# The second layer's routed experts inside the mixed stage, with stores that add their rows in memory

## The reference, cut to what matters

```python
x = x + _L0_attn_ref(xn, ...) + _L0_ffn_ref(xn, ...)
xn = _layernorm(x, axis=-1)
x = x + _L1_attn_ref(xn, ...) + _L1_ffn_ref(xn, ...)

# _L1_ffn_ref
gates = softmax(logits)                      # 8 experts
idx = argmax(gates)
locations = cumsum(mask1, axis=0) - mask1    # place of the token in its expert
mask1 = mask1 * (locations < capacity)       # capacity = 8192 / 8 = 1024
h = gelu(einsum('ecm,emi->eci', dispatched, inter_w) + inter_b)
expert_out = einsum('eci,eim->ecm', h, output_w) + output_b
moe_out = einsum('sec,ecm->sm', combine, expert_out)
out = res_mlp_out * coef[:, :1] + moe_out * coef[:, 1:] + residual
```

## Time and profile before

| | us |
|---|---|
| median of 3 runs | 1391.96 |
| lowest and highest | 1389.64, 1392.7 |
| the profiled execution | 1388.63 |
| its span in the trace | 1386.8 |

### The profile page before, as it was taken

The page is one execution under the profiler, slowest core; times in us unless marked ns, Lnnn a source line. Parts: engine busy times, 40 slices in busy tenths (PEclk is TensorE's granted clock), DMA queues, the critical chain, the costliest instruction groups (busy, mean ns, idle before and its releaser), DMA issues. The chain is left out here.

```text
span 1386.8 us, 28532 instructions
## 1 busy us (share of the span) xinstructions
PE 1158.3 (84%) x9562; PEld 856.0 (62%) x9562; DVE 1009.0 (73%) x3197; ACT 684.5 (49%) x1151; POOL 552.4 (40%) x524
## 2 busy tenths in 40 slices
PE   0771599999999997999999988999599899679980
PEld 0550255555555544899999885777366667579970
DVE  7905899999999994667666654888654688657753
ACT  1751277777777775444444334555332455334430
POOL 2300133333333331555555451333368477235550
PEclk9885699999999998999999998999799999889995
DMA  9252400000000001222222212224166000312218
GB/s 316 118 193 58 170 25 23 25 25 23 25 26 25 23 25 31 66 69 69 71 69 70 64 58 79 62 62 137 51 218 201 17 30 28 137 54 69 67 57 242
DMA packets 97340, 110.26 MB, mean 80 GB/s; under 512 B 13340, under 2 KB 84700, under 8 KB 96988
## 3 DMA queue, kind: packets, MB, share of 16 engines
q1 hardware_dynamic: 75264, 77.23, 17.7%
q0 software_dynamic: 12800, 26.63, 5.7%
q10 hardware_dynamic: 9180, 5.14, 1.2%
HBM read 59.71 MB, written 49.25 MB: 79 GB/s over the span
## 5 line engine op out<-in xcount | busy, mean ns | idle before, releaser
L1029 POOL DMA_INDIRECT slots<-rowbuf,slots x192 | 193.7, 1009 | 354.9 <-ACT probs L841 335.4
L1139 POOL DMA_INDIRECT y<-slot_y,where x208 | 217.8, 1047 | 218.5 <-DVE slot_y L1120 185.2
L841 ACT ACTIVATE probs<-ps 128x1024 f32<-128x1024 f32 x256 | 255.2, 1025 | 95.3 <-PE ps L751 95.3
L1200 ACT ACTIVATE slot_h<-ps,own 128x256 f32<-128x256 f32 x416 | 174.2, 471 | 239.8 <-PE ps L1171 237.6
L1171 PE MATMUL ps<-slot_x,own 128*128 128x256 f32 x832 | 203.5, 388 | 4.8 <-DVE slot_x L1109 3.0
L1183 PEld LDWEIGHTS ps<-own,slot_h 128*128 128x128 f32 x1664 | 203.0, 193 | 5.7 <-ACT slot_h L1200 0.3
L1183 PE MATMUL ps<-own,slot_h 128*128 128x128 f32 x1664 | 203.4, 276 | 0.0
L1171 PEld LDWEIGHTS ps<-slot_x,own 128*128 128x128 f32 x832 | 151.9, 192 | 28.2 <-DVE slot_x L1109 7.0
L767 PE MATMUL ps<-probs,vext 128*32 128x256 f32 x2048 | 136.9, 385 | 0.0
L1084 DVE COPY own<-packs 128x1156 f32 x104 | 79.5, 764 | 64.0 <-issue 54.1
L751 PE MATMUL ps<-q_stackT,k_stackT 32*128 32x256 f16 x1024 | 88.0, 275 | 0.5 <-ACT probs L841 0.2
(11 more groups left out here) (290 smaller groups left out, 2024.1 us busy)
## 6 DMA issues: line engine op xcount, KB each, us to landing
toeplitz<-conv_kernel SPq DMA_DIRECT2D x16, 1024.0 KB, 7.3
slots<-blank SPq DMA_DIRECT2D x26, 528.0 KB, 7.2
slot_rows<-slots SPq DMA_DIRECT2D x104, 132.0 KB, 2.2
routed<-y SPq DMA_DIRECT2D x48, 256.0 KB, 3.5
packs<-in_experts SPq DMA_DIRECT2D x2, 4624.0 KB, 14.1
y<-blank SPq DMA_DIRECT2D x8, 512.0 KB, 6.7
out<-stream ACTq DMA_DIRECT2D x16, 256.0 KB, 4.8
y<-slot_y,where POOLq DMA_INDIRECT x208
```

The source lines that it names most:

```text
L841: act.activation(probs[:, p % 4, :, :, :].rearrange("p j k t -> p j (k t)"), ps[:, 2 * (p % 2):2 * (p % 2) + 2, :], ACT.Exp, scale=DK ** - ...
L1029: return pool.indirect_dma_start(m["slot_dram"][layer], bass.IndirectOffsetOnAxis(ap=where, axis=0), m["rowbuf"][:, tile, :], None)
L1139: pool.indirect_dma_start(m["y_dram"][layer], bass.IndirectOffsetOnAxis(ap=where[:, j, h:h + 1], axis=0), y[:, j, h, :], None).then_inc(se ...
L1200: ins = act.activation(hidden[:, j % 2, k, :], ps[:, 2 * (j % 2) + k // 2, (k % 2) * LOT:(k % 2) * LOT + LOT], act_func, bias=own[:, j, P_ ...
```

## The change

The routed experts of layer 1 no longer have stages of their own. Their rows are handled in `middle`, behind the shared expert's groups, as 16 groups of 512 rows, two to an expert. `half(i)` now runs to 64 halves, of which those from group 16 on are routed: `make_hidden` and `make_out` take their weights from `packs[:, r // PER, :]`, without a copy. The rows of group r are loaded by SP into one of three buffers, turned by PE (`turn_rows`) into PSUM banks 4 and 5, scaled and shifted by DVE (`take_rows`), which also works out the row numbers in `out`. `put_y` adds the bias and multiplies by the weight. All buffers for it lie in `xT`, whose first columns are free by then.

SP stores `stream` to `out` as soon as a group's `added` is counted: ten groups before the expert packs, six behind the first three row loads. The packs come in eight DMAs. POOL waits until all 16 stores have landed and then sends four indirect DMAs for each group, with an addition in memory (`compute_op=ALU.add`) on the stored rows. The rows of blank slots go to three spare areas of 1024 rows behind the 8192 of `out`, which change every expert; `head` clears these (three DMAs of 512 KB) instead of `y_dram[1]`. `grouped` for layer 1 and `add_routed` are not called.

```diff
         head(nc, a, m, out)
@@ build
-            middle(nc, a, m)
-        grouped(nc, a, m, 1)
-        add_routed(nc, m, out.rearrange("(t p) d -> p t d", p=P))
+            middle(nc, a, m, out)
@@ head, SP
-            for k in range(TOKENS // rows):
-                sp.dma_start(m["y_dram"][1][rows * k:rows * (k + 1), :].rearrange("(p j) d -> p j d", p=P),
+            for k in range(SPARE):
+                first = TOKENS + k * rows
+                sp.dma_start(out[first:first + rows, :].rearrange("(p j) d -> p j d", p=P),
                              blank[:, :, 0:D]).then_inc(m["cleared"], 16)
@@ middle, SP
+            def store(g):
+                sp.wait_ge(sem["added"], g + 1)
+                sp.dma_start(final[:, tiles(g), :], stream[:, tiles(g), :]).then_inc(sem["stored"], 16)
+
+            def load_rows(r):
+                if r >= ROW_BUFFERS:
+                    sp.wait_ge(sem["y_ready"], r - ROW_BUFFERS + 1)
+                sp.dma_start(rows1[:, r % ROW_BUFFERS, :, :].rearrange("p k d -> p (k d)"), slots[r, :, :])\
+                  .then_inc(sem[f"rows{r % ROW_BUFFERS}"], 16)
+
+            for g in range(GROUPS - 6):
+                store(g)
             sp.wait_ge(sem["y_turned"], GROUPS)
-            sp.dma_start(m["packs"][:, :, :], a["experts1"][:, 0:E, :]).then_inc(m["packs_loaded"], 16)
+            for e in range(E):
+                sp.dma_start(m["packs"][:, e, :], a["experts1"][:, e, :]).then_inc(m["packs_loaded"], 16)
+            sp.wait_ge(sem["scattered"], 16 * TILES)
+            sp.wait_ge(sem["upped"], GROUPS // 2 * KI)
+            for r in range(ROW_BUFFERS):
+                load_rows(r)
+            for g in range(GROUPS - 6, GROUPS):
+                store(g)
+            for r in range(ROW_BUFFERS, GROUPS):
+                load_rows(r)
+            sp.wait_ge(sem["stored"], 16 * GROUPS)
@@ middle, POOL
             pool.wait_ge(sem["scattered"], 16 * TILES)
+            pool.wait_ge(sem["stored"], 16 * GROUPS)
+            for r in range(GROUPS):
+                pool.wait_ge(sem["y_ready"], r + 1)
+                for k in range(GROUP):
+                    pool.indirect_dma_start(
+                        out, bass.IndirectOffsetOnAxis(ap=where[:, r % SENDS, k:k + 1], axis=0),
+                        routed[:, r % SENDS, k, :], None, compute_op=ALU.add).then_inc(sem[f"sent{r % SENDS}"], 16)
+            for j in range(SENDS):
+                pool.wait_ge(sem[f"sent{j}"], 16 * GROUP * (GROUPS // SENDS))
@@ middle, PE
             def make_hidden(g):
+                r = g - GROUPS
+                if r >= 0:
+                    pe.wait_ge(sem["x_ready"], r + 1)
+                    pe.wait_ge(m["packs_loaded"], 16 + 16 * (r // PER + 1))
+                    own, x = m["packs"][:, r // PER, :], xs[:, r % 2, :]
+                else:
+                    own, x = pack, xT[:, g * GN:g * GN + GN]
...
+            def turn_rows(r):
+                pe.wait_ge(sem[f"rows{r % ROW_BUFFERS}"], 16 * (r // ROW_BUFFERS + 1))
+                if r < 2:
+                    pe.wait_ge(sem["biased"], GROUPS)
+                else:
+                    pe.wait_ge(sem["x_ready"], r - 1)
+                for k in range(GROUP):
+                    ins = pe.transpose(ps[:, ROW_TURN[r % 2], P * k:P * k + P],
+                                       rows1[:, r % ROW_BUFFERS, k, 0:D], ident)
+                ins.then_inc(sem["rows_turned"], 1)
@@ middle, PE, half
                 elif i % 2:
                     make_hidden((i + 1) // 2)
+                    if GROUPS <= (i + 1) // 2 + 1 < ALL:
+                        turn_rows((i + 1) // 2 + 1 - GROUPS)
@@ middle, DVE
+            def take_rows(r):
+                dve.wait_ge(sem["rows_turned"], r + 1)
+                if r >= 2:
+                    dve.wait_ge(sem["upped"], (GROUPS + r - 1) * KI)
+                if r >= SENDS:
+                    dve.wait_ge(sem[f"sent{r % SENDS}"], 16 * GROUP * (r // SENDS))
+                some = rows1[:, r % ROW_BUFFERS, :, :]
+                area = float(BLANK * P * (r // 2 % SPARE))
+                c.link(stt(place1[:, :], some[:, :, ROW_W2], -area, some[:, :, ROW_ID], ALU.mult, ALU.add))
+                ts(where[:, r % SENDS, :], place1[:, :], -float(TOKENS), None, ALU.add)
+                ts(xs[:, r % 2, :], ps[:, ROW_TURN[r % 2], :], nwb[:, 0:1], nwb[:, 1:2], ALU.mult, ALU.add)\
+                    .then_inc(sem["x_ready"], 1)
+
+            def put_y(r):
+                dve.wait_ge(sem["downed"], GROUPS + r + 1)
+                some = routed[:, r % SENDS, :, :]
+                tt(some, ps[:, SHARED_OUT, :].rearrange("p (k d) -> p k d", d=D),
+                   m["packs"][:, r // PER, P_OUT:PACK].unsqueeze(1).broadcast_to([P, GROUP, D]), ALU.add)\
+                    .then_inc(sem["summed"], 1)
+                dve.wait_ge(sem["summed"], GROUPS + r + 1)
+                for k in range(GROUP):
+                    ins = ts(routed[:, r % SENDS, k, :], routed[:, r % SENDS, k, :],
+                             rows1[:, r % ROW_BUFFERS, k, ROW_DW:ROW_DW + 1], None, ALU.mult)
+                ins.then_inc(sem["y_ready"], 1)
@@ middle, DVE, the list behind the 16 groups
+            take_rows(0)
+            evict(GROUPS - 2)
+            scale(GROUPS - 2)
+            scale(GROUPS - 1)
+            take_rows(1)
+            evict(GROUPS - 1)
+            for r in range(GROUPS):
+                if r + 2 < GROUPS:
+                    take_rows(r + 2)
+                put_y(r)
```

## The result

| | before | after |
|---|---|---|
| median, us | 1392.33 (1389.64 to 1393.28, 4 runs) | 1356.04 (1355.45 to 1357.14, 4 runs) |
| profiled execution | 1388.63 | 1357.14 |
| its span | 1386.8 | 1355.3 |

The ratio is 0.9758 with a 95% interval of 0.9736 to 0.9780: faster, by 36 us where 44 were forecast. The time lies in the range, 8.4 us above the predicted 1347.6. The spans of the profiled executions show more of the miss: 1355.3 against a forecast span of 1342.4, 12.9 us. The median hides 4.5 us of that by luck.

The account below looks back on a forecast made before the run. TensorE was taken to bound layer 1's routed experts, transfers the `add_routed` behind them. PE's end at 1342.4 plus 9.2 less 9.2 gave a span of 1342.4 against 1386.8; -44.4 from the median 1391.96 gave 1347.6 us, range 1334 to 1369.

Parts of the forecast that it names:

- rival (b): Head or join gives less: the head's gap has another cause (1357), or the eight expert slices don't overlap (1361); 9%.
- Part 1: Head: five fewer 512 KB clears let the DMA queue drain earlier, so `gb` and all that follows come 9.2 us earlier.
- Part 2: Mixed stage to routed experts: PE waits for first rows until 1201.35, the clock's fall costs 2.0 us, PE ends at 1329.9.
- Part 3: Routed groups: three row buffers make PE wait 0.96 us 13 times, 12.5 us; period 8.42 us, PE ends at 1342.4.
- Part 4: POOL's adding sends: taken at 1.26 us each, bounds 1.26 and 2.52; four in a period bind from 2.1 us each.
- Part 5: End: `add_routed`'s 40.3 us give way to 9.2 us from PE's end to the span's end, -31.1 us.
- (a): Routed groups: rows land within 1.6 us of the issue, so the 12.5 us of waits are gained too: 1335; 7%.
- (c): POOL becomes the bound, still faster: a send costs 2.1 to 2.6 us; at 2.52 the time is 1385; 11%.
- (d): POOL makes the kernel slower: a send costs 2.63 us or more; at 3.0 the time is 1416; 8%.
- list of signs: What the profile would show at head, join, groups, sends (0.96 busy each) and end (9 us after the last matmul).
- the join: Mixed stage to routed experts: PE idle about 6 us ahead of the first rows' transposes, released by the row DMA.
- three signs of being wrong: A send takes over 2 us, DVE waits for `sent`, or the granted clock falls in the groups for the small waits.

Follow-up runs that it names:

- e3_clears: The changed kernel with five 512 KB clears of an unused area put back in the head, ahead of the three: 1365.29 us.
- e6_onepack: The changed kernel with all eight experts' packs loaded in one DMA instead of eight: 1357.10 us.
- e2_four: The changed kernel with four row buffers instead of three: 1345.08 us.
- e1_plain: The changed kernel with plain indirect sends that overwrite, instead of adding ones: 1354.23 us.
- e5_both: The changed kernel with the edits of e2_four and e4_first together: 1340.60 us.
- e0_after: The changed kernel run once more, unaltered, beside the variants: 1356.64 us.
- e7_both_plain: e5_both with plain sends instead of adding ones: 1333.67 us.
- e4_first: The changed kernel with the first row load ahead of the expert packs, the next two between them, and a semaphore for each pack: 1355.71 us.

## Why the prediction was right, and where it was off

The number alone would not have told this forecast from rival (b), which had 1357 for a head that gives nothing. The places do: the head gave its 9 us, and the loss was at the end.

**Part 1, right.** -9.0 us at PE's restart for -9.2, and e3_clears gives it back. Whether the engines' drain or SP's issuing sets it stays open.

**Part 2, right.** First rows within 0.2 us of the forecast; the fallen clock behind the wait cost 2.1 us (0.91 and 5.23 start to start for 0.44 and 3.56) where 2.0 were taken. Rival (b) needed packs 14 us later; e6_onepack shows that the cut costs nothing.

**Part 3, mechanism right, period 0.14 too short.** 13 waits of 0.92 for 13 of 0.96. But the start-to-start time of a piece holds only where the next piece follows without a wait: ahead of a wait `make_hidden` counts with its full 3.60 us, not with the 3.46 start to start, and the turn behind it with 0.49 instead of 0.44. With 0.92 for the wait this is 8.56, 13 times 0.14 or 1.8 us in all. Another 0.88 us was missed: between the last two outputs there is no `make_hidden`, so that the second waits for `put_y(14)` to free the one bank of PSUM (the row of 1332.97). These two and the last matmul's own end (3.81 us for 3.56) are 2.9 of the 3.6 us by which PE ended late. Of parts 2 and 3, which were to bring 4 us, only 0.7 came (1336.8 against 1346.5 less 9.0). The row waits of three buffers gave back what the removed stage boundary had gained, as the forecast said, and e2_four shows them to be worth 14 us.

**Part 4, the step that failed.** The price of an adding send was taken at the nearest row, 1.26, between bounds of 1.26 and 2.52; it is 1.85, half way. The test behind that choice, "four sends in a period of 8.42 bind from 2.1 us each", is true for the groups in the middle and says nothing of the end, where the groups follow each other in 7.2 and 4.5 us. In the last of them each price above 1.13 us queues up. Even the assumed 1.26 queues there: with it, in e1_plain, the last send starts 6.1 us behind PE and not 5.7. At 1.85 POOL sends twelve times without a gap, and the end moved by 4.9 us; e1_plain takes back 4.5 of them. The landing was nearly right, 3.2 us for the 3.5 allowed. The Trainium skill has an accumulating DMA read its destination before it writes ("DMA: Bandwidth & Descriptors", "Rules for kernel authors"), and an access to memory take 0.2 us on average and 2 us at high load ("HBM Reference", "Latency", where the prediction names "Access"). The 0.9 us by which the addition lengthened the landing, from 2.3 to 3.2, lies between these figures; no run shows the read by itself. These pages have no price of an addition for the issuing engine, which is where the time went.

**Part 5, "the surest term", was off by 9.3 us.** 9.2 us were to lie between PE and the end of the span; it was 18.5. The late sends are 4.9 of it, and POOL's drain and the barrier are 4.2, which the sum left out without a reason. The trace of before had shown the drain behind just such sends. POOL's last send of layer 1's `grouped` there, and its drains from 1350 on (ns min/median/max, first and last start us):

```profile
1350.34 0.95 POOL L1139 DMA_INDIRECT y<-slot_y,where  x1 [0.30 <-DMA y<-slot_y,where]
```

```profile
L102 POOLq DRAIN  x2: 34/2654/5275, 1352.7 to 1358.7; - x2
```

The first drain, of 5.3 us, runs from 1352.7 to 1358.0, where `grouped` ends, 7.7 us after the start of the last send. It was part of the 40.3 us that the forecast took away. The sends that the forecast put in their place were given a landing but no drain, although they end on POOL in the same way. So -31.1 became -21.8.

**The rivals.** (a) is what e2_four built with a fourth buffer instead of a faster load, and got 11 us by the medians. (c) and (d) needed 2.1 and 2.63 us for a send; the price came out under both, but (c)'s mechanism is in e5_both.

**Of the list of signs**, the wait for `gb`, the join and the row waits came as written, within 0.5 us. POOL was idle between the groups, also as written. The sends (0.96) and the 9 us at the end did not. None of the three signs of being wrong came: they looked at the groups, and the error was behind them.

## What to carry to other kernels

A service engine that fits into the steady period can still set the end: take its price against the distances of the last few groups, not against the period. When the last work moves to another engine, take the drain and barrier of that engine from a stage that ends on it; the trace of before had such a stage, and it was the one that the change removed. When a new buffer ring is added, work out when its slot comes free against when the load must be issued; here the third slot came 0.9 us late thirteen times, and a fourth buffer bought 14 us.

## What the runs showed of the hardware

An indirect send with addition from POOL is 1.55 us busy and 1.85 us apart, a plain one 0.96 and 1.26. It lands in 3.2 us against 2.3. It makes 144 packets against 32, at 3.6 times the DMA share. The row loads beside it did not feel this: they landed in 2.6 us, and in 2.7 beside plain sends.

POOL's drain behind its last sends took 3.3 us after adding ones (the changed kernel and e0_after) and 5.3 us after plain ones (e1_plain, e7_both_plain, and layer 1's `grouped` before), but 3.0 us after the plain ones of layer 0's `grouped`. From the start of the last send to the end of the drain it is 7.0 us in the changed kernel and 7.8 in e1_plain. What the drain consists of is open.

Behind PE's wait of 3.08 us in e4_first the clock was down as it was behind 6.45 us in the changed kernel: 0.56 and 0.50 granted, and the next long piece at 5.40 us in both. The cost was near the lower of the forecast's bounds of 1.7 and 4 us each time: 1.8 us in e4_first (5.23 start to start for 3.44), 2.1 in the changed kernel, and 1.7 in e0_after behind 6.37 us. A wait twice as long did not cost twice as much. The 13 waits of 0.9 us in the groups left the pieces behind them at full length, 3.74 and 3.60 us.
